# Random features of a linear attention: inverse norms of four tiles at once by Newton rounds, key heads summed by accumulating transposes, three normalisations moved to ScalarE

## The reference, cut to what matters

```python
q = (x @ Wq.T + bq)   # 16 heads of 16;  k, v: 8 heads of 16, each used by two query heads
q = q * cos + rotate_half(q) * sin            # k likewise
def softmax_kernel(x, R):                     # R: 8 x 16
    n = sqrt(sum(x * x, axis=-1));  x = x / max(n, 1e-6)
    p = x @ R.T
    return concat([sin(p), cos(p)]) / sqrt(16)
qp, kp = softmax_kernel(q), softmax_kernel(k)
kv  = einsum('bhsf,bhsd->bsfd', kp, v)        # summed over the heads, token by token
out = einsum('bhsf,bsfd->bhsd', qp, kv);  out @ Wo.T + bo
```

## Time and profile before

| what | us |
|---|---|
| time before, median of 3 runs | 1104.36 (1098.37 to 1105.86) |
| span of the profiled execution | 1103.5 |
| PE busy | 1021.3 (93%) |
| PE weight loads busy | 845.2 (77%) |
| DVE busy | 711.2 (64%) |
| ACT busy | 452.3 (41%) |
| POOL busy | 431.8 (39%) |

### The profile page before, as it was taken

One profiled execution on the slowest core, in us unless ns is written; L12 is line 12 of the kernel. 1 busy time (PEld: TensorE's weight loads), 2 busy tenths in 40 slices (PEclk: granted clock), 3 DMA queues, 4 the chain that ended last, 5 costly groups with the idle time before them and its releaser, 6 DMA issues. The chain is left out here.

```text
span 1103.5 us, 18327 instructions
## 1 busy us (share of the span) xinstructions
PE 1021.3 (93%) x6383; PEld 845.2 (77%) x6383; DVE 711.2 (64%) x1740; ACT 452.3 (41%) x772; POOL 431.8 (39%) x473
## 2 busy tenths in 40 slices
PE   8889995799999999988999989999888998899997
PEld 7878885655566665577888878888778986888886
DVE  5854443988798876556554367765549977566654
ACT  4524332346675755535443312323344543223222
POOL 3246655326363621205566400000159987200000
PEclk7699997978999987888999999999988999999999
DMA  9224424200000023126542150000010300000000
GB/s 327 87 74 138 167 77 137 77 1 2 3 2 20 2 82 121 39 65 230 211 144 92 67 201 1 1 1 1 11 67 1 77 1 1 1 2 20 20 20 20
DMA packets 39179, 71.97 MB, mean 65 GB/s; under 512 B 10610, under 2 KB 28082, under 8 KB 38836
## 3 DMA queue, kind: packets, MB, share of 16 engines
q1 hardware_dynamic: 29492, 48.25, 13.3%
q0 software_dynamic: 7488, 20.46, 5.6%
q10 hardware_dynamic: 2112, 2.10, 0.6%
HBM read 46.78 MB, written 23.87 MB: 64 GB/s over the span
## 5 line engine op out<-in xcount | busy, mean ns | idle before, releaser
L2202 PE MATMUL ps<-xt,w 128*128 128x512 f32 x768 | 191.4, 399 | 4.1 <-PEq L437 2.7
L2202 PEld LDWEIGHTS ps<-xt,w 128*128 128x128 f32 x768 | 141.4, 190 | 34.4 <-DVE xt L210 4.5
L1882 DVE CUSTOM_DVE_ANT_0 ps<-ps,att_mask 128x128 f32<-128x128 f32 (+3 forms) x256 | 119.2, 517 | 28.2 <-PE ps L1440 27.8
L2296 DVE TENSOR_TENSOR had_gated<-ps,had_sig 128x512 f32<-128x512 f32 x64 | 44.3, 692 | 108.7 <-ACT had_sig L2255 108.7
L2255 ACT ACTIVATE had_sig<-ps 128x512 f32<-128x512 f32 x64 | 38.3, 599 | 185.2 <-PE ps L2202 185.2
L676 POOL DMA_INDIRECT moe_xs<-xn_rows,moe_index x78 | 85.3, 1093 | 71.1 <-DVE moe_index L1071 42.9
L1743 ACT ACTIVATE att_early_probs<-ps 128x384 f32<-128x384 f32 (+1 forms) x192 | 91.1, 528 | 51.8 <-PE ps L1455 51.2
L771 PE MATMUL ps<-moe_w,moe_narrow_xb 128*128 x390 | 110.8, 398 | 0.0
L155 POOL TENSOR_TENSOR var_eps<-bn,eps 128x4 f32<-128x4 f32 x22 | 4.7, 216 | 266.0 <-DVE bn L118 251.5
L682 POOL DMA_INDIRECT made_rows<-moe_units_made,moe_index x78 | 77.6, 995 | 71.2 <-ACT moe_units_made L919 59.6
L1331 POOL TENSOR_SCALAR_AFFINE_SELECT att_early_probs<-att_early_probs 128x256 f32<-128x256 f32 x128 | 54.6, 441 | 114.4 <-ACT att_early_probs L1743 114.1
(11 more groups left out here) (290 smaller groups left out, 2326.1 us busy)
## 6 DMA issues: line engine op xcount, KB each, us to landing
moe_w<-in_moe SPq DMA_DIRECT2D x12, 768.0 KB, 8.0
back<-made_rows SPq DMA_DIRECT2D x14, 512.0 KB, 6.3
x<-x_turned SPq DMA_DIRECT2D x8, 512.0 KB, 6.9
low_weights<-moe_w SPq DMA_DIRECT2D x4, 768.0 KB, 3.6
w_early<-in_moe SPq DMA_DIRECT2D x4, 768.0 KB, 4.5
w_early<-low_weights SPq DMA_DIRECT2D x4, 768.0 KB, 11.4
x<-in_x SPq DMA_DIRECT2D x4, 512.0 KB, 5.6
xn_rows<-moe_wide_xn SPq DMA_DIRECT2D x4, 512.0 KB, 11.4
```

Source lines behind the costliest of these rows:

```text
L1882: last = nc.vector.tensor_tensor_reduce(g.ps[:, a, col:col + n], g.ps[:, a, col:col + n], mask[:, SEQ - n:SEQ], -1.0, 3.0e38, ALU.add, ALU ...
L2202: last = nc.tensor.matmul(g.ps[:, bank(n, half), :], w[a][:, k, c * P:(c + 1) * P], xt[low][:, b % 2, k, :], start=(k == 0 and q == 0), st ...
L2296: nc.vector.tensor_tensor(gated[:, n % 2, :], g.ps[:, bank(n, 0), :], sig[:, n % 2, :], ALU.mult) \
```

## The change

The inverse norms are made for a whole group at once. PE makes the sums of squares of four tiles together (`norms`) before the group's first `tile`; DVE clamps them and makes a first guess of the inverse root from the bits of the number (`guess`, at a = 0, behind `rests`); POOL refines the 128x96 guesses in three Newton rounds of four instructions each (`refine`: two rounds at a = 0, one at a = 1, both behind `differences`), in place of sixteen powers. `angles(t)` waits for the third round of its group.

`gather` is done by accumulating transposes: 16 of 128x128 a tile in place of 8 matmuls of 128x256. The sum comes out transposed, so ACT copies it to SBUF (`summed_keys`), PE transposes it back by two more (`turn_back`), and `out_of_psum` reads that. The loop is one step longer.

Normalisations of groups 1 to 3 move from DVE to ACT (`normalise_by_scalar`), for which POOL makes two more small tensors (`rstd_and_shift`). `wholes`, `shift` and `rests` change the form of the instruction: each then has two SBUF inputs, where `wholes` and `shift` had one. `wholes` adds the large constant only, and `rests` subtracts it.

The diff, cut to its core, runs in the order of the file: the norm's helper, POOL, PE (`tile`, `norms`, `gather`, `turn_back`), ACT (whose step begins with half_sines(s+1) and half_squares(s+1) as before; `summed_keys` stands behind the squares of a = 3), DVE (`guess`, `angles`, then `wholes`, `rests`, `shift`, then the order of a step).

```diff
-    def normalise_by_scalar(self, act, b, x_block, shift, shift_done):
+    def normalise_by_scalar(self, act, b, x_block, shift, shift_done, before=0):
         nc, g, q = self.nc, self.g, self.slot(b)
-        act.wait_ge(shift_done, b + 1)
+        act.wait_ge(shift_done, b + 1 - before)
+        if b >= self.slots:
+            act.wait_ge(self.turned, b - self.slots + 1)
...
+        def inverse_of(s, a):
+
+            return s % BT == a and 0 <= (s - a) // BT + 1 < GROUPS
...
         @block.gpsimd
-            def inverse(t):
-                pool.wait_ge(clamped, t + 1)
-                if t >= 4:
-                    pool.wait_ge(turns_done, t - 3)
-                nc.gpsimd.tensor_tensor(inv_norm[:, t % 4, :], norm2[:, t % 4, :], g.neg_half[:, 0:QKH], ALU.pow) \
-                    .then_inc(inv_done, 1)
+            def refine(gr, rounds):
+                inv = inv_norm[:, gr % 2, :]
+                for n in rounds:
+                    if n == 0:
+                        pool.wait_ge(guessed, gr + 1)
+                    else:
+                        pool.wait_ge(inv_done, 3 * gr + n)
+                    nc.gpsimd.tensor_tensor(inv_square[:, :], inv, inv, ALU.mult).then_inc(newton, 1)
+                    pool.wait_ge(newton, 9 * gr + 3 * n + 1)
+                    nc.gpsimd.tensor_tensor(inv_term, inv_square[:, :], minus_half, ALU.mult) \
+                        .then_inc(newton, 1)
+                    pool.wait_ge(newton, 9 * gr + 3 * n + 2)
+                    nc.gpsimd.tensor_scalar(inv_term, inv_term, 1.5, None, ALU.add).then_inc(newton, 1)
+                    pool.wait_ge(newton, 9 * gr + 3 * n + 3)
+                    nc.gpsimd.tensor_tensor(inv, inv_term, inv, ALU.mult).then_inc(inv_done, 1)
...
             for s in STEPS:
                 gr, a = front(s)
-                if is_tile(s + 3):
-                    inverse(s + 3)
                 if is_tile(s + 2):
                     differences(s + 2)
+                if inverse_of(s, 0):
+                    refine(s // BT + 1, (0, 1))
+                elif inverse_of(s, 1):
+                    refine((s - 1) // BT + 1, (2,))
                 if a == 0 and gr:
-                    norm.rstd(pool, gr)
+                    norm.rstd_and_shift(pool, gr, minus_mean, mean_shift, mean_shifted)
...
+                if i == 0:
+                    norms(gr)
                 pe.wait_ge(roped, QK * (gr + 1))
...
-                for c in range(QK):
-                    heads = slice(N2 + c * (P // HD), N2 + (c + 1) * (P // HD))
-                    last = nc.tensor.matmul(g.ps[:, bank, heads], squares[:, c, at], head_ones[:, :],
-                                            start=True, stop=True)
+            def norms(gr):
+                bank = 2 + BT * gr % 3
+                pe.wait_ge(squared, QK * (gr + 1))
+                for i in range(BT):
+                    for c in range(QK):
+                        heads = slice(N2 + i * QKH + c * (P // HD), N2 + i * QKH + (c + 1) * (P // HD))
+                        last = nc.tensor.matmul(g.ps[:, bank, heads], squares[:, c, i * P:(i + 1) * P],
+                                                head_ones[:, :], start=True, stop=True)
+                last.then_inc(norms_ps, 1)
...
-                for k in range(HKV):
-                    last = nc.tensor.matmul(g.ps[:, 5 + t % 2, 0:D], g.ident[:, :],
-                                            wv_prod[:, t % 2, k, :, :].rearrange("p h d -> p (h d)"),
-                                            start=(k == 0), stop=(k == HKV - 1))
+                for half in range(KC):
+                    for k in range(HKV):
+                        row = wv_prod[:, t % 2, k, half * (H // 2):(half + 1) * (H // 2), :]
+                        last = nc.tensor.matmul(g.ps[:, 5 + t % 2, half * P:(half + 1) * P],
+                                                row.rearrange("p h d -> p (h d)"), g.ident[:, :], is_transpose=True,
+                                                start=(k == 0), stop=(k == HKV - 1))
                 last.then_inc(ctx_ps, 1)
+            def turn_back(t):
+                pe.wait_ge(keys_out, t + 1)
+                for half in range(KC):
+                    last = nc.tensor.transpose(g.ps[:, 5 + t % 2, D + half * P:D + (half + 1) * P],
+                                               over_keys[:, t % 2, half, :], g.ident[:, :])
+                last.then_inc(keys_back, 1)
             for s in STEPS:
                 gr, a = front(s)
+                if is_tile(s - 2):
+                    turn_back(s - 2)
                 if (a == 0 or gr is None) and is_tile(s - 1):
                     gather(s - 1)
...
         @block.scalar
+            def summed_keys(t):
+                act.wait_ge(ctx_ps, t + 1)
+                if t >= 2:
+                    act.wait_ge(keys_back, t - 1)
+                nc.scalar.activation(over_keys[:, t % 2, :, :].rearrange("p k n -> p (k n)"), g.ps[:, 5 + t % 2, 0:D],
+                                     ACT.Copy).then_inc(keys_out, 1)
...
+                if is_tile(s - 2):
+                    out_of_psum(s - 2)
                 elif a == 1 and gr:
+                    norm.normalise_by_scalar(act, gr, x_tile(gr), mean_shift, mean_shifted, 1)
                     tables(gr)
...
-                if is_tile(s - 2):
-                    out_of_psum(s - 2)
+                if is_tile(s - 1):
+                    summed_keys(s - 1)
...
         @block.vector
+            def guess(gr):
+                dve.wait_ge(tile_ps, BT * gr + 1)
...
+                sums_of_squares = g.ps[:, 2 + BT * gr % 3, N2:N2 + BT * QKH]
+                nc.vector.tensor_scalar(norm2[:, :], sums_of_squares, 1e-12, None, ALU.max).then_inc(clamped, 1)
+                nc.vector.tensor_scalar(minus_half, sums_of_squares, 1e-12, -0.5, ALU.max, ALU.mult) \
+                    .then_inc(clamped, 1)
+                dve.wait_ge(clamped, 2 * gr + 2)
+                nc.vector.tensor_scalar(inv_norm[:, gr % 2, :].bitcast(I32), norm2[:, :].bitcast(I32),
+                                        -0.5, float(0x5f3759df), ALU.mult, ALU.add).then_inc(guessed, 1)
...
-                dve.wait_ge(inv_done, t + 1)
+                dve.wait_ge(inv_done, 3 * (t // BT + 1))
...
-                nc.vector.tensor_scalar(whole[:, t % 2, :, :], turns[:, t % 2, :, :], ROUND, ROUND,
-                                        ALU.add, ALU.subtract).then_inc(whole_done, 1)
+                nc.vector.tensor_tensor(whole[:, :, :], turns[:, t % 2, :, :],
+                                        round_to[:, :].unsqueeze(2).to_broadcast([P, QKH, HALF]), ALU.add) \
+                    .then_inc(whole_done, 1)
+                nc.vector.scalar_tensor_tensor(out=rest[:, t % 2, :, :], in0=whole[:, :, :], scalar=ROUND,
+                                               in1=turns[:, t % 2, :, :], op0=ALU.subtract, op1=ALU.subtract) \
+                nc.vector.scalar_tensor_tensor(out=flat, in0=f32(g.ones[:, 0:1]).to_broadcast([P, HKV * H]),
+                                               scalar=-HALF / 2.0, in1=flat, op0=ALU.mult, op1=ALU.add).then_inc(shifted, 1)
...
-                if is_tile(s + 3):
-                    clamp(s + 3)
                 if is_tile(s + 2):
                     rests(s + 2)
+                if inverse_of(s, 0):
+                    guess(s // BT + 1)
                 if is_tile(s):
                     weigh(s)
                 if a == 0 and gr:
                     norm.stats(dve, gr, x_tile(gr))
-                elif a == 1 and gr:
-                    norm.normalise(dve, gr, x_tile(gr))
```

51 lines of the change are left out of this document (29 added, 22 removed).

## The result

| | time, median | ratio to before, 95% interval |
|---|---|---|
| before | 1102.91 us (1098.37 to 1105.86, 4 runs) | |
| after | 1124.25 us (1118.22 to 1131.07, 4 runs) | 1.0211 (1.0169 to 1.0253) |

Slower by 2.1%, where +0.5% was forecast and 1121 was the upper end. The four executions after lie in two pairs: 1118.22 and 1118.55 us, with a mean granted clock of 0.925 and 0.922, and 1129.95 and 1131.07 us, both with 0.912. The profile is that of the first, which by itself lies inside the forecast's range; the second pair has no profile.

What follows compares the result with a forecast made beforehand. PE was taken to set the pace at 29.65 us a group. From 1104.4 us: start -0.8, projection rounds +5.1, last steps 0, end -0.8, clock +2, giving 1109.9 us; range 1094 to 1121.

Steps and rivals of the forecast that it cites:

- The two projection rounds: Two rounds of four tiles, 828 to 889 us: a group goes from 29.65 to 32.2 us, +5.1 us in all.
- The wait ahead of `angles`: At a = 1 DVE idles 4.45 us once a group, while POOL does differences and then the third Newton round.
- The 2.05 at a = 0: At a = 0 differences starts ahead of weigh and holds it, so 2.05 us a group are lost.
- a held `wholes`: At a = 0 the first Newton rounds meet wholes on DVE: 0.3 us more a group.
- The last eight steps: Steps after the projections, 44.3 us before: waits and shorter steps sum to 44.35, no change.
- The start: Up to the end of group 1's rotations: -0.8 us, with bounds of -2.5 and +1.5.
- The end: From the last weigh to ACT's last copy: 3.4 us in place of 4.2, so -0.8.
- The clock: PE idles some 8 us in 32, its clock falls: between 0 and 10.5 us lost, 2 taken.
- The signs: For right: differences' median over 4 us, angles waiting 4 to 5, weigh behind differences, PE 23 to 25 busy, POOL down 10 to 20.
- The first (no collisions): Rival: weigh and differences run side by side on DVE and POOL; -11.6 us, 1092.8 us; chance 17%.
- the fourth: Rival: an accumulating transpose costs 0.22 us or ACT's longer chain holds PE; PE 31.1 a group, 1113 us; 6%.
- The second: Rival: PE's clock falls and stays low for much of the stage; +8.5 over the 2 taken, 1118.4 us; 22%.

Runs made afterwards that it cites:

- filled_clock: The changed kernel with 30 matmuls of 128x128 that nobody reads added on PE in steps 1 and 5; 1123.39 us, ratio 1.021 to before.
- transposes_again: The kernel before with only the gather by accumulating transposes, measured a second time; 1098.04 us, ratio 0.997 to before.
- newton_only: The kernel before with the Newton part alone (norms, guess, rounds), old gather, normalisation and instruction forms; 1126.70 us, ratio 1.023 to before.
- all_but_newton_home: Changed kernel with norms and next tile before turn-back and gather at a = 0, round 3 before differences, normalisation on DVE; 1113.52 us, ratio 1.013 to before.

## Why the prediction was wrong

The direction held, and the mechanism in part; two terms of the sum were too small. The stage, forecast at +5.5, took +16.0. The profiled execution, 1118.2 us, still lay in the range; with the pair at 1130 us the median did not, and what made that pair slower no profile shows.

1. **The two projection rounds** had +5.1 us and took +12.9 (5.4 and 7.5). This is the step that failed, in two places. **The wait ahead of `angles`**, "2.36 + 2.0 + 0.1 = 4.45", was 6.05: I wrote that "POOL is idle when `rests` ends". At a = 1 it isn't; the last operation of round 2 is held by `weigh`, and the four small operations of the deviation follow it. My own count of POOL's work (1.8 us a group for these) never met the order of its queue. **The 2.05 at a = 0** was put on `differences` holding `weigh`. In group 2 it did so to the hundredth; in group 3 `guess` waited 4.58 us for PE, and `differences` ran inside that wait. I followed the norms on PE for group 0 only, where no gathers are ahead of them. `weigh` held the first Newton operation (2.33 in place of 0.35).
   The sum had also compared unlike things: 29.65 before is a period with its waits, 32.2 after is work and collisions alone. Waits for squares, 0.83 and 1.23 after, were in the first and not in the second (before had 0.63 and 1.68), and by the marks the groups before were 28.5 and 29.6. So two groups came to 71.0 where 64.4 was forecast: 3.2 of it ahead of `angles`, 2.1 net at a = 0 and 2.1 for squares, less 0.6 priced for a held `wholes` that did not come; the last 1.2 of the miss lie in the 59.3 used for before, where the marks give 58.1.
2. **The last eight steps**, forecast at no change, took 47.5 us against 44.3: the same two terms, 4.16 ahead of `guess` (2.05 priced) and 5.44 ahead of `angles` (4.45 priced), 3.1 together. The steps between them were as written: `differences` 4.3 to 4.4 us, `wholes` 1.12.
3. **The start** (forecast -0.8) came to -0.1, from the first rotation to the end of group 1's (28.96 and 28.89 us). **The end** (-0.8): from the last `weigh`'s start to the last copy's end 6.48 before, 6.42 after, as PE still had the tile before it in hand.
4. **Right sizes:** DVE's work of a group, 25.4 (25.35 and 25.06 busy), with some luck, as the 27.5 it starts from is one window's and between the marks DVE was busy for 26.9; a Newton round of 1.8 to 1.9 (2.0 forecast), operations of 0.35 to 0.45; 16 accumulating transposes in 1.91 us, 0.109 for each but the pipeline's fill; PE at 22.7 to 25.3 busy us in 32 to 34. **The clock** (+2) fell, to 0.79; the waits for squares were no longer than before, and filled_clock gives 1.6 and 2.1 us a group for a rise to 0.95 and 0.90.
5. **The signs.** Of those for "right", `weigh` behind `differences` and PE's busy time came; the wait of `angles` was longer than 4 to 5, POOL's busy sum fell by 21.5 (10 to 20 forecast), and `differences` had a median of 3.37 us, not over 4, since eight of the sixteen were not held.
6. **The rivals.** The first (no collisions) is refuted: `differences` beside `weigh` takes 4.34 to 4.40 us in eight steps, each ending 2.2 behind its `weigh`. Its sum has a slip: 40.2 against 44.3 is -4.1 and not "about -6", which gives 1094.7. In the fourth, 18 records at 0.22 us make PE 31.4 a group and not 31.1. The second came near in size (1118.4) with the wrong cause: the clock was low, but raising it gave little. What the page "SBUF — State Buffer" of the Trainium skill says under "Who interferes with whom" is borne out both ways here, down to an operation over 4 elements. The power is an exception: in the kernel before, one over 128x24 began at 880.04 and `weigh` at 880.56, and both kept their normal lengths, 4.18 and 2.28 us. So "whoever comes first runs alone" was too wide. Of the page "TensorE: Matmul & The Clock Gate", "Part 4: PE-mode transpose", these runs can say little. With the whole gather in transposes, transposes_again had a granted clock of 1.00 and 0.94 from 829 to 890 us and 0.73 from 890 to 922, the last steps, where before had 1.00; but PE was busy for 21.7 of these 32 us, against 34.9 of 40 before. And newton_only had 0.81 and 0.79 without these transposes.

Not settled: why the median after is 21 us above before when the stage holds 16 of them and the rest of the profiled execution shows none; what lets the clock fall; and how much of the fall from 122.6 to 113.0 in all_but_newton_home is the order and how much the normalisation's place.
